# The end of a three-layer kernel: the flag's branch, the last chunks' statistics and the last copies rearranged

## The chip, the cores and the metric
The kernel runs on one core of one Trainium2 chip. The metric is the time of one execution on the device in microseconds (us), taken as the median of several runs. A profile of one execution comes with it; its span runs from the first to the last instruction that belongs to the kernel.

## The reference, cut to what matters
The input is x, 4 batches of 2048 tokens of 256 numbers. Three layers are added to it one after the other:

```python
x = x + 0.5 * ffn(layernorm(x), gate_w, w1, b1, w2, b2)
x = x + attn(layernorm(x), Wq, Wk, Wv, Wo)
x = x + 0.5 * ffn(layernorm(x), gate_w, w1, b1, w2, b2)

# ffn: 8 experts, two of them chosen for each token
cap = int(1.25 * N / E)                       # 1280
probs = softmax(x @ gate_w.T); top2_w, top2_idx = top_k(probs, 2)
counts = bincount(top2_idx.reshape(-1), length=E)
keep = counts <= cap                          # an expert with more tokens than cap gives nothing
# attn: 16 heads of 16, each query sees keys within 128, and token 0 sees and is seen by all
```

An expert that more than 1280 of the 16384 choices fall to adds nothing at all. So if all eight experts are over the limit, both ffn layers add zero, and the result is x + attn(layernorm(x)).

## The kernel before, in words
The kernel computes the attention on the bet that no expert is kept, and collects on the way what is needed to see whether the bet holds: the gates' logits of all tokens before the attention (`logits[0]`), and those after it (`logits[1]`) for the first three batches. From these, eleven VectorE operations (ROUTE, L1299) and a matmul with three small operations (COUNT, L1009 and L1333) make one number, `any_kept`. After the attention every engine loads that number (L1510) and branches on it. If it is 0, nothing is left to do. If not, the general path follows: `route`, `experts`, and perhaps the attention once more. With this input the number is 0.

The attention works on groups: 4 batches of 4 groups of 4 heads, 16 groups, each of 16 tiles of 128 tokens. One tile of a group is an item; the program counts time in quarters of an item, 256 quarters for a batch. Each event has a quarter at which it is begun, read from tables such as `OUT_AT`, and every engine issues its instructions in the order of the quarters (`stages` and `schedule`). An event waits on semaphores for what it needs; the order itself is fixed.

For every item TensorE computes the scores twice. A (L951) serves the row maxima, taken by VectorE (L1447). B (L985) is turned into probabilities by ScalarE (L1128), whose band edges GpSimd cuts (L1237, L1242). PV (L1003) multiplies them by the values into `o_bank`. After every fourth item the bank is copied to `o_raw` (COPY_OUT: ScalarE L1141, and VectorE L1368 for the last six of the 64 quartets), turned by TensorE (TURN, L1023), and added, divided and stored in `attn` by VectorE (OUT_ADD, OUT_RECIP, OUT_MULT: L1476, L1483, L1494).

When all groups of a batch are done, its tokens go through a last stage in 4 chunks of 512 ("LATE"): TensorE turns `attn` (TURN_ATTN, L809, two halves p = 0 and 1), a copy brings it to `attnT` (ScalarE L1069; VectorE L1360 for the last batch), TensorE projects it (PROJECT, L823, four tiles), VectorE adds the residual in `x_ring` (L1355), SyncE stores the chunk (L750). For the second layer's logits VectorE also takes each tile's mean and variance (MOMENTS, L1287 and L1289), and GpSimd derives the logits (RSTD, L1155 to L1185). The four chunks of the last batch have start quarters of their own (`LATE_AT_END`), and the rest of the plan in common with the other batches (`LATE`).

PSUM has eight banks: three for A, two for B, one for PV's sums, and two (`misc`) that TURN, TURN_ATTN, PROJECT, the projections of the next batch (QK, VALUES), the turning of the maxima (L961) and the first token's row (FIRST, L884 among it) share. Which of the two banks a piece gets follows from the order of the quarters: the one that was emptied first.

At the end of the attention's block SyncE waits until all stores have landed (L751 to L754). The block ends with a barrier of all engines (L680), `reset()` follows with another barrier that clears the semaphores (L154), then the load of the flag and the branch.

Of the kernel before, what the change touches and what calls it, by code (L numbers as in the profile page):

```python
# [48 lines left out]
def build(nc, x, wqk, wback, wv, wo, gate, w1, b1, w2, b2, consts, x1, out):  # L49
    ctx = ExitStack()  # L50
    with ctx:
# [318 lines left out]
        def window(j):  # L370
# [19 lines left out]
        OPENING = {'ORDER_HEADS': -55, 'WBACK': -52, 'FOLD': 174, 'K_ONES': 45,  # L390
                   'FILL': 20, 'QK_APART': 1, 'STACK': 4, 'STACKS': 12}
        LATE_AT = (99, 115, 131, 146)
        LATE_AT_END = (51, 66, 83, 100)
        LATE = {'LOAD': -6, 'TURN_ATTN': 1, 'PROJECT': ((7, 8, 10, 10), (12, 12, 14, 14)),
                'BASE': 0, 'MOMENTS': (12, 17, 19, 21), 'RSTD': 23, 'STORE': 19}
        OUT_AT = (0, 0, 3, 3, 0, -1, -1, 0, 2, -1, 1, 0, 0, 0, 3, 4)
        OUT = {'TURN': 0, 'ADD': 0, 'RECIP': 1, 'MULT': 1}
        MAX_AT = {'KEY0': -1, 'TURN_MAX': 1, 'MAX': 2, 'PIECES': 3, 'P0': -1, 'EXP0': 6}

        def stages(nb, first):  # L400
# [15 lines left out]
            for b in range(nb):  # L416
                for c in range(4):
                    early = BATCH * b + EARLY_AT[c] if b else EARLY_AT_OPENING[c]
                    late = BATCH * (b + 1) + (LATE_AT if b < nb - 1 else LATE_AT_END)[c]
                    order.append((early + EARLY["MOMENTS"][0], "EARLY", b, c, early))  # L420
                    order.append((late + LATE["MOMENTS"][0], "LATE", b, c, late))
            order = [item[1:] for item in sorted(order, key=lambda item: item[0])]
            for i, (phase, b, c, at) in enumerate(order):
                plan = EARLY if phase == "EARLY" else LATE
                end(at + plan["LOAD"] if b or phase == "LATE" else -96, "LOAD", i)
                if phase == "LATE":
                    for p in range(2):
                        begin(at + LATE["TURN_ATTN"], "TURN_ATTN", i, p)
                        opening(at + LATE["TURN_ATTN"] + 1, "TURN_ATTN_IN", i, p)
                        for part, quarter in enumerate(LATE["PROJECT"][p]):  # L430
# [4 lines left out]
                    end(at + LATE["BASE"], "BASE", i)  # L435
                    end(at + LATE["STORE"], "STORE", i)
                for t in range(4):
                    quarter = plan["MOMENTS"][t]
                    if (phase, b, c) == ("LATE", nb - 1, 3):
                        quarter = LATE["PROJECT"][t // 2][KC * (t % 2) + KC - 1] + 1  # L440
                    end(at + quarter, "MOMENTS", i, t)
                end(at + plan["RSTD"], "RSTD", i)
# [58 lines left out]
            if first:  # L501
# [10 lines left out]
            return order, opens, begins, ends  # L512

        ROUTE_OPS = 11
# [56 lines left out]
        def attend(nb, dram, batch_at, tiles_at, first):  # L571
# [104 lines left out]
            def stacked(x):  # L676

                return 16 * STACK_DMAS * (x // 4 + 1)

            with nc.Block() as block:  # L680
                @block.sync
                def _(sp):
# [346 lines left out]
                def _(act):  # L1029
# [4 lines left out]
                    for kind, *n in events:  # L1034
# [28 lines left out]
                        elif kind == "TURN_ATTN_IN" and not drained(kind, n[0]):  # L1063
# [80 lines left out]
                def _(pool):  # L1144
                    for kind, *n in events:
                        if kind == "RSTD":
                            i, = n
                            phase, b, c, _ = order[i]
                            tiles = slice(4 * c, 4 * c + 4)
                            pool.wait_ge(S["moments_ready"], 4 * i + 4)  # L1150
                            if i:
                                pool.wait_ge(S["shift_ready"], i)
                            if i >= 2 and order[i - 2][0] == "EARLY":
                                pool.wait_ge(*normed(i - 2))
# [442 lines left out]
```

## Time and profile before

| what | us |
|---|---|
| median of 3 runs | 867.27 |
| lowest and highest of them | 866.34, 868.48 |
| the profiled execution, its own time | 864.91 |
| span of its profile | 862.9 |

The profile lists for each engine its busy time and each group of equal instructions. PE is TensorE, PEld its weight load, DVE VectorE, ACT ScalarE, POOL GpSimd, SP SyncE. A letter q behind an engine's name (PEldq, SPq) means its sequencer: waits, barriers, branches and the issue of transfers. A gap before an instruction stands in square brackets, with what ended it behind the arrow. L with a number is the line of the kernel.

### The profile page before, as it was taken

To read this page: it belongs to the slowest core of one execution; us is meant where nothing else is said; L and a number is where in the kernel's file an instruction comes from. 1 tells how busy PE (TensorE), PEld (TensorE's weight loads), DVE (VectorE), ACT (ScalarE), POOL (GpSimd) and SP (SyncE) were. 2 spreads that over 40 slices of the span, in tenths; PEclk is the share of its full clock that TensorE was granted. 3 is DMA by queue.
4 is the path that set the end of the run, shared out by engine and by line. 5 is a ranking of instruction groups with operands and counts; after the bars stand their busy time and mean duration, and the time that the engine had idled before them with its cause. 6 is when DMAs were issued, how large, how long until landed. Compare 5 with 4: busy or idle time off the path is not lost.

```text
span 862.9 us, 50601 instructions
## 1 busy us (share of the span) xinstructions
PE 816.7 (95%) x21504; PEld 609.6 (71%) x21505; DVE 751.2 (87%) x2814; ACT 633.3 (73%) x1416; POOL 487.2 (56%) x874
## 2 busy tenths in 40 slices
PE   9798999999999999999999999999999999999894
PEld 8555667677777777667778777667777777766672
DVE  7798799998987899998988799998988789999865
ACT  2248978998777667898777676899777756788850
POOL 3212556775554466766555465866554455756863
PEclk9899999999999999999999999999999999999998
DMA  7531224342213334342222344442222244220122
GB/s 230 98 94 64 68 76 130 96 126 64 84 54 98 110 110 159 116 129 64 87 67 70 97 127 140 148 108 85 70 77 64 95 119 140 92 74 31 55 67 87
DMA packets 93190, 83.50 MB, mean 97 GB/s; under 512 B 17568, under 2 KB 92192, under 8 KB 92960
## 3 DMA queue, kind: packets, MB, share of 16 engines
q1 hardware_dynamic: 91360, 78.91, 29.9%
q8 instruction: 171, 2.80, 1.4%
q10 hardware_dynamic: 1600, 1.31, 0.9%
q14 instruction: 59, 0.48, 0.2%
HBM read 20.66 MB, written 8.39 MB: 34 GB/s over the span
## 4 chain that ended last, share of the span: by engine, by line
PE 69%; DVE 12%; ACT 11%; issue 4%; POOL 2%; DMA 1%; SPq 1%; POOLq 0%; ACTq 0%; DVEq 0%
PE bank L1003 13%; PE bank L951 12%; PE bank L985 11%; PE bank L840 11%; PE bank L855 6%; PE bank L823 5%; DVE bank L1447 5%; ACT probs L1128 5%; PE bank L1023 3%; PE bank L809 2%; PE bank L761 2%; ACT pieces L1078 1%; PE bank L776 1%; DVE stats L1287 1%; ACT k_stack L1132 1%
## 5 line engine op out<-in xcount | busy, mean ns | idle before, releaser
L1128 ACT ACTIVATE probs<-bank 128x384 f32<-128x384 f32 (+1 forms) x1024 | 459.5, 481 | 142.1 <-PE bank L985 125.3
L1447 DVE CUSTOM_DVE_ANT_0 bank<-bank,con 128x288 f32<-128x288 f32 x1024 | 494.8, 519 | 55.9 <-PE bank L951 47.7
L951 PE MATMUL bank<-k_stack,q_stack 96*32 96x288 bf16 x4096 | 326.2, 289 | 9.9 <-DVE row_max L1447 6.0
L985 PE MATMUL bank<-q_stack,k_stack 99*32 99x288 bf16 (+2 forms) x4096 | 319.4, 284 | 11.6 <-ACT probs L1128 7.3
L1003 PE MATMUL bank<-probs,v_sb 128*32 128x128 f32 x5888 | 305.6, 272 | 4.1 <-issue 1.4
L1237 POOL TENSOR_SCALAR_AFFINE_SELECT probs<-probs 128x512 f32<-128x512 f32 x240 | 155.0, 646 | 174.8 <-ACT probs L1128 174.4
L1003 PEld LDWEIGHTS bank<-probs,v_sb 128*32 128x32 f32 x5888 | 193.0, 110 | 38.1 <-issue 5.2
L951 PEld LDWEIGHTS bank<-k_stack,q_stack 96*32 96x32 bf16 x4096 | 127.1, 96 | 73.3 <-DVE row_max L1447 21.0
L985 PEld LDWEIGHTS bank<-q_stack,k_stack 99*32 99x32 bf16 x4096 | 123.9, 94 | 70.5 <-ACT probs L1128 44.5
L1242 POOL TENSOR_SCALAR_AFFINE_SELECT probs<-probs 128x512 f32<-128x512 f32 x240 | 153.4, 639 | 19.2 <-ACT probs L1128 19.2
L840 PE MATMUL bank<-xnT,wqk_sb 128*32 128x256 f32 x2048 | 161.5, 386 | 0.6 <-DVE neg_max L1469 0.5
L1447 DVE DVE_READ_ACCUMULATOR2_ANT row_max<- 128x1 f32 x1024 | 145.2, 142 | 0.0
L1225 POOL TENSOR_TENSOR pieces<-rest,pieces 128x512 bf16<-128x512 f32 x64 | 74.5, 1163 | 63.1 <-ACT pieces L1093 61.0
L855 PE MATMUL bank<-wv_sb,xnT 128*32 128x272 f32 x1024 | 83.5, 393 | 1.7 <-ACT v_sb L1100 1.1
L823 PE MATMUL bank<-wo_sb,attnT 128*32 128x264 f32 x1024 | 72.7, 386 | 2.3 <-DVE attnT L1360 1.0
L840 PEld LDWEIGHTS bank<-xnT,wqk_sb 128*32 128x32 f32 x2048 | 65.5, 112 | 6.5 <-ACT v_sb L1100 1.2
L1078 ACT ACTIVATE pieces<-bank 128x512 bf16<-128x512 f32 x64 | 38.3, 598 | 24.3 <-PE bank L840 23.5
L1375 DVE TENSOR_TENSOR rest<-bank,pieces 128x512 f32<-128x512 f32 x64 | 44.1, 689 | 4.1 <-ACT pieces L1078 3.9
L1287 DVE BATCH_NORM_STATS2 stats<-x_ring 128x6 f32<-128x256 f32 x112 | 47.2, 421 | 0.2
L1093 ACT ACTIVATE pieces<-rest 128x512 bf16<-128x512 f32 x64 | 40.6, 634 | 7.6 <-DVE rest L1375 7.5
L1023 PE MATMUL bank<-con,o_raw 128*32 128x68 f32 x2048 | 44.1, 223 | 1.4 <-ACT o_raw L1141 1.0
L823 PEld LDWEIGHTS bank<-wo_sb,attnT 128*32 128x32 f32 x1024 | 33.5, 109 | 14.6 <-issue 2.6
(123 smaller groups left out, 730.9 us busy)
## 6 DMA issues: line engine op xcount, KB each, us to landing
q_stack<-pieces SPq DMA_DIRECT2D x384, 64.0 KB, 2.7
k_stack<-pieces SPq DMA_DIRECT2D x364, 64.0 KB, 2.7
x_ring<-in_x SPq DMA_DIRECT2D x28, 512.0 KB, 4.9
out_x<-x_ring SPq DMA_DIRECT2D x16, 512.0 KB, 4.1
attn<-in_x SPq DMA_DIRECT2D x4, 512.0 KB, 5.8
wback_sb<-in_wback SPq DMA_DIRECT2D x8, 256.0 KB, 6.3
k_stack<-pieces ACTq DMA_DIRECT2D x20, 64.0 KB, 3.6
q_stack<-neg_max SPq DMA_DIRECT2D x48, 16.0 KB, 2.2
```

Of the source, the lines that this page charges most:

```text
L823: last = pe.matmul(bank_of("PROJECT", i, t)[SP * s:SP * (s + 1), 0:D + E], attnT[:, t // 2, k, at:at + SP], wo_sb[:, k, :], start=(k == 0) ...
L840: last = pe.matmul(bank_of("QK", g, c)[SP * s:SP * (s + 1), 256 * half:256 * (half + 1)], wqk_sb[:, g % NG, k, SP * s:SP * (s + 1)], xnT[: ...
L855: last = pe.matmul(bank_of("VALUES", b, t)[SP * s:SP * (s + 1), 0:D + HD], xnT[:, k, at:at + SP], wv_sb[:, k, :], start=(k == 0), stop=(k ...
L951: last = pe.matmul(a_ring[i % len(a_ring)][SP * s:SP * (s + 1), 0:WIN], q_stack[g % 2][0:KROWS, h, q:q + SP], k_stack[g % 2][0:KROWS, h, q ...
L985: last = pe.matmul(score_bank(i)[SP * s:SP * (s + 1), start:final], k_stack[g % 2][0:SROWS, h, WINDOW + P * j + SP * s:WINDOW + P * j + SP ...
L1003: last = pe.matmul(o_bank[SP * h:SP * (h + 1), P * (i % 4):P * (i % 4 + 1)], v_sb[:, j, VW * head:VW * head + SP], probs[:, j % 4, h, P * ...
L1023: last = pe.matmul(bank_of("TURN", n)[SP * s:SP * (s + 1), HG * VW * i:HG * VW * (i + 1)], o_raw[:, at:at + SP], take, start=True, stop=True)
L1128: act.activation(probs[:, j % 4, h, c0:c1], score_bank(i)[:, c0:c1], ACT.Exp, scale=LOGIT_SCALE).then_inc(S["exp_ready"], 1)
L1225: pool.tensor_tensor(pieces[i % 2][:, 2, :], rest[:, :], pieces[i % 2][:, 1, :], ALU.subtract).then_inc(S["piece3_ready"], 1)
L1237: pool.affine_select(out=part, in_=part, compare_op=ALU.is_ge, fill=0.0, base=0, pattern=[[0, HG], [1, P]], channel_multiplier=-1).then_in ...
L1242: pool.affine_select(out=part, in_=part, compare_op=ALU.is_ge, fill=0.0, base=0, pattern=[[0, HG], [-1, P]], channel_multiplier=1).then_in ...
L1447: dve.tensor_tensor_reduce(out=a_ring[i % len(a_ring)][:, 0:WIN], in0=a_ring[i % len(a_ring)][:, 0:WIN], in1=mask, scale=1.0, scalar=con[: ...
```

## The change
- The statistics (MOMENTS) and logits (RSTD) of chunks 1, 2 and 3 of the last batch are no longer computed in the attention. They are computed in the general path (`take_left_out`), which the branch enters only if an expert is kept. `any_kept` doesn't use them.
- SyncE's wait for the stores leaves the attention's block. It stands now in the Else branch of the flag, and in `take_left_out`. The `reset()` after the attention goes; one stands at the end of either branch.
- The last COPY_OUT and the first half of the last chunk's copy to `attnT` are ScalarE's.
- The last batch has a plan of its own, `LATE_END`, with new quarters for its loads, turns, projections, statistics and stores; `LATE_AT_END`, `OUT_AT` (used in every batch), the routing's start and the count's place get new numbers.

The code of MOMENTS and RSTD moves into the functions `moments` and `deviations` without other edits.

```diff
-        LATE_AT_END = (51, 66, 83, 100)
+        LATE_AT_END = (52, 68, 85, 102)
         LATE = {'LOAD': -6, 'TURN_ATTN': 1, 'PROJECT': ((7, 8, 10, 10), (12, 12, 14, 14)),
                 'BASE': 0, 'MOMENTS': (12, 17, 19, 21), 'RSTD': 23, 'STORE': 19}
-        OUT_AT = (0, 0, 3, 3, 0, -1, -1, 0, 2, -1, 1, 0, 0, 0, 3, 4)
+        LATE_END = {'LOAD': -22, 'TURN_ATTN': 0, 'PROJECT': ((6, 6, 8, 9), (12, 15, 15, 15)),
+                    'BASE': -2, 'MOMENTS': (12, 16, 16, 23), 'RSTD': 35, 'STORE': 24}
+        COUNT_AT = 16
+        OUT_AT = (0, 0, 0, 3, -1, -1, -1, 3, 0, 3, 1, 0, 0, 0, 3, 0)
...
+        def left_out(first, nb, phase, b, c):
+            return first and phase == "LATE" and b == nb - 1 and c > 0
...
-                plan = EARLY if phase == "EARLY" else LATE
+                plan = EARLY if phase == "EARLY" else LATE if b < nb - 1 else LATE_END
...
-                for t in range(4):
+                for t in range(0 if left_out(first, nb, phase, b, c) else 4):
...
-                end(at + plan["RSTD"], "RSTD", i)
+                if not left_out(first, nb, phase, b, c):
+                    end(at + plan["RSTD"], "RSTD", i)
...
-                at = BATCH * nb + 7
+                at = BATCH * nb + ROUTE_AT          # 6
...
-                end(max(at + 4 * ROUTE_OPS, BATCH * nb + 4 * LAG_B) + 4, "COUNT")
+                end(max(at + 4 * ROUTE_OPS, BATCH * nb + 4 * LAG_B) + COUNT_AT, "COUNT")
...
             def drained(kind, n):       # true: VectorE copies, false: ScalarE
                 if kind == "COPY_OUT":
-                    return 4 * n + 3 + LAG_PV > NT * NG * nb
-                return order[n][1] == nb - 1
+                    return 4 * n + 3 + LAG_PV > NT * NG * nb and n < 4 * NG * nb - 1
+                return order[n[0]][1] == nb - 1 and (order[n[0]][2] < 3 or n[1] == 1)
...
+            def take_left_out():
+                kept = [i for i, (phase, b, c, _) in enumerate(order) if left_out(first, nb, phase, b, c)]
+                with nc.Block() as block:
+                    @block.sync
+                    def _(sp):
+                        await_stores(sp)
+                    @block.vector
+                    def _(dve):
+                        for i in kept:
+                            for t in range(4):
+                                moments(dve, i, t)
+                    @block.gpsimd
+                    def _(pool):
+                        for i in kept:
+                            deviations(pool, i)
+                reset()
...
-                    for m in range(3):
-                        laps = [lap for s, lap in store_of.values() if s is S[f"stored{m}"]]
-                        if laps:
-                            sp.wait_ge(S[f"stored{m}"], max(laps))
+                    if not first:
+                        await_stores(sp)
...
+            if first:
+                return await_stores, take_left_out
             reset()
...
-        attend(B, x, ..., True)
+        await_stores, take_left_out = attend(B, x, ..., True)
         any_expert = nc.values_load(any_kept[0:1, 0:1], min_val=0, max_val=1)
         with nc.If(any_expert != 0):
-            reset()
+            take_left_out()
             route(logits[0], flags_of[0])
...
+            reset()
+        with nc.Else():
+            await_stores(nc.sync)
             reset()
```

## Rows read from the trace of the kernel before

**Rows 1.** The page, busy time, share of the span and number of instructions.
```profile
PE 816.7 (95%) x21504; PEld 609.6 (71%) x21505; DVE 751.2 (87%) x2814; ACT 633.3 (73%) x1416; POOL 487.2 (56%) x874
```

**Rows 2.** TensorE's waits, whole span: us in total, times, longest.
```profile
PE bank L1023 <- ACT o_raw L1141: 1.0, 5, 0.3
...
PE bank L884 <- DVE attn L1494: 1.0, 3, 0.3
```

**Rows 3.** Timeline of TensorE from 841: start us, us, instructions merged.
```profile
840.80 0.84 PE L1003 MATMUL bank<-probs,v_sb 128*32 128x128 f32 x24
842.19 1.99 PE L823 MATMUL bank<-wo_sb,attnT 128*32 128x264 f32 x32 [0.55 <-DVE attnT L1360]
844.80 1.10 PE L823 MATMUL bank<-wo_sb,attnT 128*32 128x264 f32 x16 [0.63 <-DVE x_ring L1355]
845.69 0.69 PE L1023 MATMUL bank<-con,o_raw 128*32 128x68 f32 x32
846.54 1.10 PE L823 MATMUL bank<-wo_sb,attnT 128*32 128x264 f32 x16 [0.16 <-DVE x_ring L1355]
847.78 1.12 PE L809 MATMUL bank<-con,attn 128*128 128x128 f32 x8
849.39 4.20 PE L823 MATMUL bank<-wo_sb,attnT 128*32 128x264 f32 x64 [0.50 <-DVE attnT L1360]
```

**Rows 4.** Busy time of TensorE in one stretch: us, busy (instructions), clock, DMA.
```profile
841.64:853.59 11.95, 9.91 (x169) 1.00 0.31 100
```

**Rows 5.** Timeline of VectorE, 840 to 854.
```profile
840.78 0.16 DVE L1335 TENSOR_SCALAR within<-bank 1x16 f32<-1x16 f32 x1 [0.85 <-PE bank L1013]
...
841.35 1.29 DVE L1360 COPY attnT<-bank 128x512 f32<-128x512 f32 x2
...
843.64 0.67 DVE L1368 COPY o_raw<-bank 128x512 f32<-128x512 f32 x1
...
853.93 0.40 DVE L1355 TENSOR_TENSOR x_ring<-bank,x_ring 128x264 f32<-128x264 f32 x1
```

**Rows 6.** Groups of equal instructions on VectorE from 840 to 855.1.
```profile
L1287 DVE BATCH_NORM_STATS2 stats<-x_ring 128x6 f32<-128x256 f32 x10 | 4.2, 419 | 0.2
```

**Rows 7.** Timeline of GpSimd from 855.
```profile
855.10 0.23 POOL L1155 TENSOR_SCALAR var_eps<-mean_var 128x4 f32<-128x4 f32 x1 [1.59 <-DVE mean_var L1289]
...
857.35 0.24 POOL L1185 TENSOR_TENSOR all_logits<-late_move,rstd 128x32 f32<-128x32 f32 x1
```

**Rows 8.** Waits of SyncE from 850.
```profile
SPq L680 <- DMA out_x<-x_ring: 2.5, 1, 2.5
```

**Rows 9.** The store's line from 800: duration ns min/median/max, first and last start.
```profile
L750 SPq DMA_DIRECT2D out_x<-x_ring x4: 383/384/384, 829.5 to 854.4; - x4
...
DMA to landing us min/median/max: 2.9/3.6/4.4
```

**Rows 10.** Lines of the end, same columns: block's barrier, clearing barrier, branch.
```profile
L680 SPq COMPARE_BRANCH  x1: 43/43/43, 857.4 to 857.4; - x1
L680 SPq DRAIN  x1: 7/7/7, 857.5 to 857.5; - x1
...
L680 PEldq EVENT_SEMAPHORE  x1: 51/51/51, 857.8 to 857.8; - x1
...
L154 PEldq EVENT_SEMAPHORE  x1: 51/51/51, 858.7 to 858.7; - x1
...
bacc.py:44 PEldq COMPARE_BRANCH  x1: 3454/3454/3454, 859.5 to 859.5; - x1
...
bacc.py:44 SPq COMPARE_BRANCH  x1: 45/45/45, 859.6 to 859.6; - x1
```

**Rows 11.** ScalarE's copies to o_raw in the body, same columns.
```profile
L1141 ACT ACTIVATE o_raw<-bank x58: 591/593/605, 98.7 to 792.4; 128x512 f32<-128x512 f32 x58
```

**Rows 12.** Timeline of SyncE and TensorE from 798.
```profile
800.74 1.09 SPq L712 DMA_DIRECT2D x_ring<-in_x  x2
...
806.56 0.43 PE L1003 MATMUL bank<-probs,v_sb 128*32 128x128 f32 x8 [1.41 <-issue]
```

More of the change, by code:

```diff
@@ L427, in stages @@
                     for p in range(2):
-                        begin(at + LATE["TURN_ATTN"], "TURN_ATTN", i, p)
-                        opening(at + LATE["TURN_ATTN"] + 1, "TURN_ATTN_IN", i, p)
-                        for part, quarter in enumerate(LATE["PROJECT"][p]):
+                        begin(at + plan["TURN_ATTN"], "TURN_ATTN", i, p)
+                        opening(at + plan["TURN_ATTN"] + 1, "TURN_ATTN_IN", i, p)
+                        for part, quarter in enumerate(plan["PROJECT"][p]):
                             t, k = divmod(part, KC)
@@ L507, in stages @@
                     opening(OPENING["FOLD"] + 16 * half + 1, "FOLD_IN", half)
[L508 removed]
+                at = BATCH * nb + ROUTE_AT
                 for op in range(ROUTE_OPS):
                     end(at + 4 * op, "ROUTE", op)
[L511 removed]
+                end(max(at + 4 * ROUTE_OPS, BATCH * nb + 4 * LAG_B) + COUNT_AT, "COUNT")
             return order, opens, begins, ends
+        ROUTE_AT = 6
         ROUTE_OPS = 11
@@ L678, in stacked, with moments @@
                 return 16 * STACK_DMAS * (x // 4 + 1)
+            def moments(dve, i, t):
+                phase, b, c, _ = order[i]
+                if t == 0 and phase == "EARLY":
+                    dve.wait_ge(*x_loaded(i))
+                if t == 0 and i >= 2:
+                    dve.wait_ge(S["shift_ready"], i - 1)
+                if phase == "LATE":
+                    dve.wait_ge(*emptied("PROJECT", i, t))
+                if 4 * i + t >= 4:
+                    dve.wait_ge(S["moments_ready"], 4 * i + t - 3)
+                dve.bn_stats(stats[:, t, :], x_tiles(i)[:, t, :]).then_inc(S["stats_ready"], 1)
+                dve.wait_ge(S["stats_ready"], 4 * i + t + 1)
+                dve.bn_aggr(mean_var[:, i % 2, t, :], stats[:, t, :]).then_inc(S["moments_ready"], 1)
@@ new lines, in await_stores @@
+            def await_stores(sp):
+                for m in range(3):
+                    laps = [lap for s, lap in store_of.values() if s is S[f"stored{m}"]]
+                    if laps:
+                        sp.wait_ge(S[f"stored{m}"], max(laps))
+            def take_left_out():
[14 more added lines that the diff above has]
+                reset()
@@ L1062, in _ @@
                                            ACT.Copy).then_inc(free_sem("XT", i, p), 1)
-                        elif kind == "TURN_ATTN_IN" and not drained(kind, n[0]):
+                        elif kind == "TURN_ATTN_IN" and not drained(kind, n):
                             i, p = n
@@ L1146, in _ @@
                         if kind == "RSTD":
[L1147 to L1154, printed above, removed]
@@ L1155, in _ @@
-                            pool.tensor_scalar(var_eps[:, :], mean_var[:, i % 2, :, 1], EPS, None, ALU.add)\
-                                .then_inc(S["eps_added"], 1)
-                            if phase == "EARLY":
-                                if b >= 2:
-                                    pool.wait_ge(S["shift_ready"], late_index[b - 2, c] + 1)
-                                pool.tensor_scalar(neg_mean[:, b % 2, tiles], mean_var[:, i % 2, :, 0], -1.0, None,
-                                                   ALU.mult).then_inc(S["move_ready"], 1)
@@ L1188, in _ @@
+                            deviations(pool, *n)
                         elif kind == "FILL":
@@ L1276, in _ @@
                         if kind == "MOMENTS":
[L1277 to L1289 removed]
+                            moments(dve, *n)
                         elif kind == "NORM" and on_vector(n[0]):
@@ L1356, in _ @@
                                .then_inc(free_sem("PROJECT", i, t), 1)
-                        elif kind == "TURN_ATTN_IN" and drained(kind, n[0]):
+                        elif kind == "TURN_ATTN_IN" and drained(kind, n):
                             i, p = n
```

98 lines of the change are left out of this document (50 added, 48 removed).

## The prediction
> **What bounds the kernel now.** First the busy shares: TensorE is busy for 816.7 of 862.9 us [rows 1], so in the body an edit on another engine pays only where it removes a TensorE wait. The list of TensorE's waits says how little is there around the output turns, the pieces of the body that are moved: eight waits of at most 0.3 us, 2.0 us together [rows 2]. The end is another stage. The last multiplications with the probabilities (L1003) end at 840.80 + 0.84 = 841.64, and no attention is left but four pieces of chunk work: project chunk 2 (L823, four tiles), turn the last output quartet (L1023), turn chunk 3 (L809), project chunk 3 [rows 3]. The table of stretches shows TensorE busy for only 9.91 of the 11.95 us from 841.64 to 853.59 [rows 4]; each gap is named in the timeline: 0.55 for attnT, 0.63 and 0.16 for x_ring (a bank to be emptied), about 0.15 before the turn of chunk 3, 0.50 for attnT again [rows 3]. All of them are VectorE. Its timeline shows why: it waits 0.85 us for the count (L1335) before it may copy attnT at 841.35, copies o_raw only at 843.64 although its input was complete at 841.64, and ten statistics, 4.2 us [rows 6], stand with their aggregates between its copies [rows 5]. The last addition ends at 853.93 + 0.40 = 854.33.
>
> From 854.33 to 862.9 no matrix work is left, 8.6 us. Two things run side by side first: GpSimd's last deviations, from 855.10 to 857.59 [rows 7], and the last store, issued at 854.4 for 0.38 us [rows 9]; SyncE waits 2.5 us for its landing [rows 8] and leaves that wait at 857.4. Then comes a chain of single steps [rows 10]: the block's barrier lets TensorE go at 857.8, the barrier that clears the semaphores at 858.7, the flag is loaded, and TensorE's branch over the unused experts starts at 859.5 and takes 3.454 us, to 862.9. Outside the span lie 864.91 - 862.9 = 2.0 us.
>
> **The change, part by part.** *Work between 841.64 and 854.33.* Twelve statistics and twelve aggregates (chunks 1 to 3) and three sets of deviations go; ten of each stand in the stretch read above. I worked out TensorE's new order from the new quarter numbers, counted from the last batch's end at 1024: turn chunk 2 at 85, last multiplications to 90, project tile 0 at 91, the last output turn at 92, tile 1 at 93 and 94, the count at 96, tiles 2 and 3 at 97 to 100, turn chunk 3 at 102, its tiles at 108 to 119. Let E be the end of the last multiplications.
> - Tile 0, E to E+1.0: its attnT was turned before, and the count no longer stands ahead of VectorE's copy, so the 0.55 wait goes.
> - Output turn, E+1.0 to E+1.7: the copy of o_raw is now ScalarE's, which is idle after its last exponential, at 0.593 us [rows 11]; it is there by E+0.75. If ScalarE were not free, it would cost 0.67 on VectorE [rows 5].
> - Tile 1 to E+2.7, the count 0.2, tile 2 needs the bank of the output turn, which VectorE frees after its add, reciprocal and multiply (about 1.3 us with issue) at E+3.0: a gap of 0.2. Tile 3 to E+5.05; nothing stands before its bank now.
> - Turn of chunk 3: its first half follows at once, the second waits for the addition of tile 3 (0.43 + 0.15 of hand-over): gap 0.1; end E+6.25.
> - Copies of attnT: ScalarE takes the first half while TensorE turns the second, so projecting starts near E+6.45, a gap of 0.2 in place of 0.50.
> - Four tiles at 4.20/4 each (the 4.20 us row shows them back to back, so here nothing is won), to E+10.65; hand-over 0.15 and addition 0.40: E+11.2.
>
> Before, that distance was 854.33 - 841.64 = 12.7. Gain 1.5; with the count (0.2) no longer ahead of E, less than that since it comes back behind E: I take 1.6 in all. The lower bound is 0.2 (only the statistic that delays the last addition, which could start at 853.59 + 0.15 and starts at 853.93); the upper one is all idle time, 11.95 - 9.91 = 2.0, plus those 0.2. What is late next is TensorE itself, at 1.05 us a tile. GpSimd ends early: its last set is gone.
>
> *End.* SyncE no longer waits in the block. From the last addition's end: issue done +0.5 (854.4 + 0.38 - 854.33), block's end on SyncE +0.1, barrier +0.45 (857.4 to 857.8 [rows 10]), then without the clearing barrier the flag load and the branch, 858.7 to 862.9 = 4.2; then in the Else branch SyncE's wait, long met (the store lands at about +3.0, the branch ends at +5.25), and the clearing barrier, 857.8 to 858.7 = 0.9. Sum 6.15 in place of 8.6: gain 2.4. The clearing barrier has only moved; what is won is landing and deviations, which the load and the branch now cover. Two things no row shows. What SyncE's drain at the block's end does with a store in flight: in the rows it took 7 ns after the landing, so 0 to 2.5; I take 0, since that 7 ns row is the nearest. And a branch beside store traffic: 3.454 on idle queues is the one row, so 0 more to another 3.454 if the Else's few instructions need a second fetch; I take 0, since the one row shows one fetch.
>
> The Trainium skill ("Runtime: NRT & Kernel Launch", Instruction fetch mechanics) says that a taken branch whose target lies outside the two pages held forces a fetch by DMA before anything runs. The 3.454 us row on TensorE agrees; the 45 ns row on SyncE shows the branch alone. Against the change speaks "Trainium Kernel Development and Optimization", Key Constraints: transfers of all queues share the same 16 DMA engines and interleave; by it the fetch, now beside a 512 KB store, would be longer than 3.45, and the sum smaller by the part of the store that is still to move.
>
> *The loads* go from 6 to 22 quarters ahead, so three follow at 800.74 instead of two [rows 12]; behind them on SyncE stand only stores. Chunk 3's load waits for chunk 0's store (landing 2.9 to 4.4 [rows 9]) ahead of chunk 1's store: neither is near the end. Right after the two loads TensorE stands 1.41 us for nothing that is named [rows 12]. A third load may lengthen that by half (0.7) or leave it; I take 0.
>
> *The body.* Six of sixteen output turns move by 1 to 4 quarters in each of four batches, 24 in all. The one moved from 0 to -1 stands where others have waits on o_raw (five, 1.0 together, at most 0.3 [rows 2]): 4 x 0.2 = 0.8 lost. The one moved from -1 to 3 gets out of the way of the first-row matmuls (L884 waits for attn three times, 1.0 together [rows 2]): 1.0 won. The others trade places between banks. I take 0, with -2 and +2 as ends; the deviation of one set from quarter 74 to 87 and the routing one quarter earlier lie beside TensorE's 95% [rows 1] and count nothing; uncovered, a set would be the 2.5 us between the last statistic and 857.59.
>
> Sum: 1.6 + 2.4 = 4.0 on a profiled execution of 864.91, which lies 2.4 below the median of 867.27; taken off that median: 863.3.
>
> **Rivals.** *The drain or the fetch gives the end back*: either the landing is waited for after all, and of the end's 2.4 nothing is left (865.7), or the fetch takes 1.5 longer beside the store (864.8) or comes twice (866.7). For it: neither case is in the trace. Against: the drain's 7 ns, and one branch row that already includes one fetch. *The reordered tail does not pay*: a bank claimed in the new order by the wrong piece leaves the waits; 1.6 falls to 0.2, 864.7. *The body gains too*: the 1.0 at L884 without the losses, and part of the gaps beside the other moved turns; 2 us more, 861.3. *Slower*: the moved output turns each wait, or make their bank's next user wait, 0.33, what the three at L884 are [rows 2]: 24 x 0.33 = 7.9, 867.3 - 4.0 + 7.9 = 871.2. It decides from (4.0 + 2.6)/24 = 0.27 a turn. Against: there are two banks, and most turns at the same offsets show no wait in the list.
>
> **How the numbers follow.** A measurement of this kernel tells about 0.3% (2.6 us) from no change: faster is under 864.7. Forecast (gain 3 to 5, 862.3 to 864.3): 0.52. Drain or fetch: 0.16, nearly all "same". Tail does not pay: 0.10, on the border, a third of it faster. Body gains too: 0.15. Slower: 0.07. Faster 0.52 + 0.15 + 0.03 of the border case = 0.70; same 0.23; slower 0.07. The range leaves out the slower case and the tip of the best: 860.8 to 866.7.
>
> **What would show it.** Right: between the last L1003 and the last addition about 11.2 us with TensorE idle under 1 us; the copy of o_raw on ScalarE within 0.8 us of E; the block's barrier released about 1.0 us after the last addition; a branch near 3.45 us, then one clearing barrier, the span's end 6.2 us after the last addition. Wrong: SyncE's drain ends only with the landing; a branch over 4.5 us or two of them; L1023, L884 or L961 with more waits than before in the middle batches; a gap well over 1.41 us at 805.

## The result and the profile after

The changed kernel takes 860.79 us (median), the kernel before 867.27: the ratio is 0.9923, with an interval from 0.9895 to 0.995, that is 6.7 us less (4.3 to 9.1). The forecast was 863.3, the range 860.8 to 866.7: the sign was right, the gain is 6.7 where 4.0 were forecast, and the time lies 0.01 us below the range. The profiled execution took 860.79 us, its span is 858.7.

Below, E is again the end of the last multiplications with the probabilities (L1093 in the new file), T the end of the last addition (L1393).

Busy shares on the page of the changed kernel, against [rows 1]:
```profile
PE 811.9 (95%) x21504; PEld 611.7 (71%) x21505; DVE 743.2 (87%) x2788; ACT 634.7 (74%) x1418; POOL 481.3 (56%) x856
```
TensorE's timeline after E, changed kernel, against [rows 3]:
```profile
839.79 0.62 PE L1093 MATMUL bank<-probs,v_sb 128*32 128x128 f32 x16
840.22 1.07 PE L913 MATMUL bank<-wo_sb,attnT 128*32 128x264 f32 x16
841.12 0.68 PE L1113 MATMUL bank<-con,o_raw 128*32 128x68 f32 x32
842.04 1.10 PE L913 MATMUL bank<-wo_sb,attnT 128*32 128x264 f32 x16 [0.24 <-DVE x_ring L1393]
842.93 0.25 PE L1103 MATMUL bank<-counts,ones 128*1 128x8 f32 x4
843.22 1.99 PE L913 MATMUL bank<-wo_sb,attnT 128*32 128x264 f32 x32
845.14 1.33 PE L899 MATMUL bank<-con,attn 128*128 128x128 f32 x8
846.57 3.82 PE L913 MATMUL bank<-wo_sb,attnT 128*32 128x264 f32 x64
```
ScalarE's timeline there, and VectorE's last addition (against [rows 5]):
```profile
840.47 0.60 ACT L1231 ACTIVATE o_raw<-bank 128x512 f32<-128x512 f32 x1 [5.47 <-PE bank L1093]
845.83 0.60 ACT L1159 ACTIVATE attnT<-bank 128x512 f32<-128x512 f32 x1 [4.76 <-PE bank L899]
```
```profile
850.45 0.43 DVE L1393 TENSOR_TENSOR x_ring<-bank,x_ring 128x264 f32<-128x264 f32 x1 [0.46 <-PE bank L913]
```
E is 839.79 + 0.62 = 840.41 and T is 850.88: 10.5 us in place of 12.7. Of the five gaps that the prediction read from [rows 3] one of size is left, 0.24 before tile 1, which waits for tile 0's addition; before the last four tiles 0.1 is left (846.47 to 846.57). ScalarE has o_raw copied 0.66 after E.

The lines of the end (ns min/median/max, first and last start), against [rows 10]: the block's barrier, the flag's load, the branch, the Else branch's wait for the stores, the clearing barrier.
```profile
L772 SPq DRAIN  x1: 128/128/128, 851.4 to 851.4; - x1
...
L772 PEldq EVENT_SEMAPHORE  x1: 51/51/51, 851.7 to 851.7; - x1
```
```profile
L1550 SPq TENSOR_LOAD <-any_kept x1: 1092/1092/1092, 851.8 to 851.8; - x1
...
L1550 PEldq TENSOR_LOAD <-any_kept x1: 1079/1079/1079, 851.8 to 851.8; - x1
L1550 SPq FUSED_REGOPS  x1: 194/194/194, 852.9 to 852.9; - x1
L1550 SPq SEQ_ASSERT  x1: 37/37/37, 853.1 to 853.1; - x1
```
```profile
L1567 PEldq COMPARE_BRANCH  x1: 3382/3382/3382, 853.0 to 853.0; - x1
L1567 SPq COMPARE_BRANCH  x1: 50/50/50, 853.5 to 853.5; - x1
```
```profile
L750 SPq EVENT_SEMAPHORE  x2: 17/22/28, 857.9 to 857.9; - x2
```
```profile
L154 PEldq DRAIN  x1: 78/78/78, 856.4 to 856.4; - x1
...
L154 PEldq EVENT_SEMAPHORE  x1: 51/51/51, 858.7 to 858.7; - x1
```
SyncE's drain takes 128 ns with the store in flight, and the barrier opens at 851.7, 0.8 after T: the landing is not waited for. But TensorE is at the clearing barrier at 856.4, and SyncE executes its first instruction of the Else branch only at 857.9. The distance from T to the span's end is 7.8; the forecast was 6.15, and before it was 8.6.

Ahead of E something else is to be seen. TensorE's waits over the whole span, changed kernel (total, times, longest), against [rows 2]:
```profile
PE bank L1093 <- issue: 4.8, 5, 3.0
...
PE bank L1051 <- DVE attn L1532: 1.6, 2, 0.8
...
PE bank L1113 <- ACT o_raw L1231: 1.6, 8, 0.3
```
The waits of the first row's matmuls (L884) on attn are gone; the turn of the maxima (L1051) waits instead. And the stand (idle time of TensorE that no semaphore explains, "issue") of 1.41 near 806 [rows 12] is 3.0 now. The first line is TensorE's timeline, the second SyncE's. The third is the table of stretches for the 6.8 us behind the stand: length, busy time and number of instructions of PE, PEld, DVE, ACT and POOL, then TensorE's granted clock, the DMA engines' share and GB/s.
```profile
804.39 0.66 PE L1093 MATMUL bank<-probs,v_sb 128*32 128x128 f32 x8 [3.01 <-issue]
```
```profile
796.93 2.19 SPq L804 DMA_DIRECT2D x_ring<-in_x  x3
```
```profile
804.39:811.20 6.81, 6.80 (x148) 5.73 (x151) 3.41 (x6) 3.36 (x9) 2.98 (x5) 0.56 0.03 6
```
After standing 3 us TensorE works at a granted clock of 0.56: most of that stretch at the lower level (1.2 GHz). This trace is the worst one: behind the stands of 2.5 us or more at this place in the other traces of this document the clock of such a stretch is 0.75 to 0.80, behind the shorter ones 1.00 in all but one.

One trace is one execution. In the table stand the means of all traces of the kernel before (six) and of the changed kernel and two near copies of it (five in all; body_back and loads_back, below), in us. "First exp" is the first exponential of a group.

| stage | before | after | difference |
|---|---|---|---|
| start to first exp | 75.7 | 76.0 | +0.3 |
| to first exp of group 14 | 694.7 | 692.6 | -2.1 |
| to first exp of group 15 | 33.5 | 32.6 | -0.8 |
| to E | 38.3 | 39.8 | +1.5 |
| E to T | 12.7 | 10.5 | -2.2 |
| T to the span's end | 8.7 | 7.8 | -0.9 |
| span | 863.6 | 859.3 | -4.3 |

The third, fifth and sixth differences are steady, since these stages vary by 0.5 at most in nearly all traces. The exception is one trace of the kernel before whose stand near 801 fell into the third stage (34.4); the other five have 33.3, so that this difference is -0.7 without it. The first, second and fourth move by up to 4, 5 and 3 us between executions of the same kernel.

### The profile page after: what moved, and what is told of

It reads as the page before. It is cut to its first block, busy times and chain, and to the rows that moved or that the text cites. A ratio compares the mean times of both kernels' runs of the same rounds, so it can differ in the third digit from the quotient of the medians.

```text
span 858.7 us, 50541 instructions
## 1 busy us (share of the span) xinstructions
PE 811.9 (95%) x21504; PEld 611.7 (71%) x21505; DVE 743.2 (87%) x2788; ACT 634.7 (74%) x1418; POOL 481.3 (56%) x856
## 4 chain that ended last, share of the span: by engine, by line
PE 67%; DVE 13%; ACT 9%; issue 4%; SPq 2%; DMA 2%; POOL 1%; ACTq 0%; DVEq 0%
PE bank L1093 14%; PE bank L1075 11%; PE bank L1041 11%; PE bank L930 10%; PE bank L945 6%; PE bank L913 6%; DVE bank L1485 6%; ACT probs L1218 4%; PE bank L1113 3%; PE bank L899 2%; DVE stats L698 1%; SPq L830 1%; ACT xn L1131 1%; PE bank L866 1%; DVE row_max L1485 1%
## 5 line engine op out<-in xcount | busy, mean ns | idle before, releaser
L1075 PE MATMUL bank<-q_stack,k_stack 99*32 99x288 bf16 (+3 forms) x4096 | 320.3, 286 | 11.4 <-ACT probs L1218 8.3
L1093 PE MATMUL bank<-probs,v_sb 128*32 128x128 f32 x5888 | 307.6, 273 | 6.0 <-issue 4.8
L1093 PEld LDWEIGHTS bank<-probs,v_sb 128*32 128x32 f32 x5888 | 194.2, 111 | 38.4 <-issue 8.2
L930 PE MATMUL bank<-xnT,wqk_sb 128*32 128x256 f32 x2048 | 157.7, 379 | 0.6 <-DVE neg_max L1507 0.5
L1168 ACT ACTIVATE pieces<-bank 128x512 bf16<-128x512 f32 x64 | 38.3, 598 | 20.3 <-PE bank L930 19.1
L1304 POOL TENSOR_TENSOR glob_term<-v_all,p 128x272 f32<-128x272 f32 x64 | 41.6, 649 | 2.2 <-DVE v_all L1454 1.8
```

The source lines that it names most:

```text
L930: last = pe.matmul(bank_of("QK", g, c)[SP * s:SP * (s + 1), 256 * half:256 * (half + 1)], wqk_sb[:, g % NG, k, SP * s:SP * (s + 1)], xnT[: ...
L1075: last = pe.matmul(score_bank(i)[SP * s:SP * (s + 1), start:final], k_stack[g % 2][0:SROWS, h, WINDOW + P * j + SP * s:WINDOW + P * j + SP ...
L1093: last = pe.matmul(o_bank[SP * h:SP * (h + 1), P * (i % 4):P * (i % 4 + 1)], v_sb[:, j, VW * head:VW * head + SP], probs[:, j % 4, h, P * ...
```

## The experiments

Each ratio is to runs of the kernel before taken beside it on the same chip.

**Which part pays.** The kernel before again; the changed kernel again; the new end alone; the statistics alone (left out altogether in this kernel, and so not computed in the general path either); statistics and end together with the old order and copies; the changed kernel with its last copies on VectorE.
```diff
 end_only:    LATE_AT_END, OUT_AT, ROUTE_AT, COUNT_AT, drained as before; LATE_END = LATE
+             left_out(...): return False
 stats_only:  (in the kernel before)
+             left_out = first and phase == "LATE" and b == nb - 1 and c > 0
 stats_end:   tables and drained as before, left_out as in the change
 copies_old:
-             return 4 * n + 3 + LAG_PV > NT * NG * nb and n < 4 * NG * nb - 1
-             return order[n[0]][1] == nb - 1 and (order[n[0]][2] < 3 or n[1] == 1)
+             return 4 * n + 3 + LAG_PV > NT * NG * nb
+             return order[n[0]][1] == nb - 1
```


> The kernel before, unchanged, as a yardstick for what differs from execution to execution. Theory A (the clock in the opening differs by chance): ratio to the kernel before 1.000; its profile shows in the first 80 us another number of stretches at the lower clock than the profile of before had (0.76 granted from 26 to 40 us), and the first exponential lies elsewhere than 77.6 us. Theory B (the opening differs because of the change): the first exponential is at 77.6 again, and the granted clock from 26 to 40 is 0.76 again.

> The changed kernel unchanged, for a second profile and more times. Both theories: 10.48 us from the last multiplications to the last addition, 7.7 from there to the end, ratio 0.992. Theory A (the differences ahead of the last multiplications are chance): the start of the first exponential differs from 74.0 by the number of stretches at the lower clock in the opening, and TensorE's stand near 801 is sometimes near 1.3 us instead of 3.0. Rival (the stand belongs to the changed code): 3.0 us again.

> The kernel before with one part of the change: the wait for the stores and the clearing barrier go behind the branch. Statistics, order and copies are the old ones. Theory A (GpSimd's last deviations end the block at 857.6 as before, the landing at 857.4 was just hidden by them): barrier, load, branch and clearing barrier in another order, 8.6 us from the last addition to the span's end as before, ratio 1.000, less 0.4 us at most. Rival (the landing alone was the price): 2 us faster, 0.9975.

> The kernel before without the statistics and deviations of the last batch's chunks 1 to 3; order, copies and end are the old ones. It leaves those statistics out altogether (the general path, which this input doesn't enter, would lack them). Theory A (what the traces show behind the last multiplications is the whole gain, the rest is chance before it): 12.69 us from the last multiplications to the last addition falls to about 11.7 (the waits for x_ring go, those for attnT stay), 8.55 us from there to the span's end to 8.3, since the landing is waited for; ratio 0.9985. Theory C (the missing statistics also take something away ahead of the last multiplications, in the executions that are timed): ratio 0.995 or lower.

> The kernel before with the statistics of chunks 1 to 3 moved to the general path and with the new end (wait for the stores and clearing barrier behind the branch); tables, order and copies are the old ones. Theory A: last multiplications to last addition as without the statistics (about 11.7 us), from there 7.7 us as in the changed kernel; ratio 0.998. Theory C: ratio 0.994. What it lacks to the changed kernel is the new order and ScalarE's copies.

> The changed kernel with all of the last copies on VectorE again. Theory A: the wait of the output turn grows by 0.2 to 0.4 us and the one before chunk 3's projection to about 0.5, so 10.48 us become 11.0 and the kernel is 0.5 us slower than the changed one, ratio to the kernel before about 0.993. Rival (the copies on ScalarE are idle detail): 10.48 us stay.

| kernel | us | ratio, 95% | E to T | T to end |
|---|---|---|---|---|
| before_again | 865.28 | 1.000 (0.9974 to 1.0026) | 12.69 | 8.54 |
| end_only | 867.18 | 0.9992 (0.9961 to 1.0023) | 12.69 | 9.78 |
| stats_only | 865.35 | 0.998 (0.9957 to 1.0003) | 11.17 | 8.72 |
| stats_end | 864.11 | 0.9975 (0.9948 to 1.0001) | 11.17 | 7.85 |
| copies_old | 861.36 | 0.9932 (0.9907 to 0.9957) | 10.67 | 8.20 |
| after_again | 860.94 | 0.9912 (0.9879 to 0.9944) | 10.48 | 8.07 |

The distance from E to T is the same to 0.02 in all traces of one order, and so it splits cleanly: the statistics 1.52, the new order 0.50, the copies on ScalarE 0.19. The statistics are worth more than was expected of stats_only (11.7), the copies less than was expected of copies_old (11.0). TensorE's stretch in stats_only, against [rows 3]:
```profile
847.59 0.68 PE L1025 MATMUL bank<-con,o_raw 128*32 128x68 f32 x32
848.44 1.10 PE L825 MATMUL bank<-wo_sb,attnT 128*32 128x264 f32 x16 [0.16 <-DVE x_ring L1357]
...
851.18 3.82 PE L825 MATMUL bank<-wo_sb,attnT 128*32 128x264 f32 x64 [0.38 <-DVE attnT L1362]
```
Without the statistics the 0.63 before the output turn is gone, and the last four tiles take 3.82 in place of 4.20: the row of 4.20 held waits behind the statistics that it did not list. In copies_old the last tiles still wait 0.20 for attnT, the price of VectorE's copy:
```profile
843.89 3.82 PE L913 MATMUL bank<-wo_sb,attnT 128*32 128x264 f32 x64 [0.20 <-DVE attnT L1398]
```
The new end alone wins nothing: GpSimd's deviations still end 3.25 us behind T and hold the block, and the Else branch then puts SyncE's late arrival and a clearing barrier behind it (9.78). It needs the statistics gone.

**What the end costs.** The wait for the landing back in the block; and the flag loaded without its check against 0 and 1.
```diff
 landing_waited:
-                    if not first:
-                        await_stores(sp)
+                    await_stores(sp)
 no_assert:
-        any_expert = nc.values_load(any_kept[0:1, 0:1], min_val=0, max_val=1)
+        any_expert = nc.values_load(..., skip_runtime_bounds_check_because="...")
```


> The changed kernel with SyncE's wait for the stores inside the attention's block again; all else is the changed one. Theory A (the landing runs beside barrier, load and branch, and the flag's load takes 1.1 instead of 0.5 us because the store is in flight): load 0.5 us, 9.8 us from the last addition to the span's end instead of 7.8, 2 us slower than the changed kernel. Rival (what ends last is not the landing, so nothing is won by taking it out): 7.8 us stay.

> The changed kernel without SyncE's check of the flag's bounds between its load and its branch. Theory A (SyncE branches 0.5 us after the others, and its code comes 4.2 us later, so it is the last at the clearing barrier): SyncE's branch 0.5 us earlier, 7.8 us become 7.3, 0.5 us faster than the changed kernel, which is less than the runs can tell apart, so the trace decides. Rival (SyncE's code comes when the other four have theirs, whenever it asks): 7.8 us stay.


Measured: landing_waited 861.85 us, 0.9955 (0.9933 to 0.9977), T to the end 9.75; no_assert 860.78 us, 0.9945 (0.9923 to 0.9966), T to the end 6.85. Flag loads of landing_waited, where the store has landed before:
```profile
L1549 SPq TENSOR_LOAD <-any_kept x1: 479/479/479, 852.8 to 852.8; - x1
...
L1549 PEldq TENSOR_LOAD <-any_kept x1: 486/486/486, 852.8 to 852.8; - x1
```
SyncE's branch and its first instruction behind it, no_assert (its T is 853.91):
```profile
L1568 SPq COMPARE_BRANCH  x1: 50/50/50, 855.9 to 855.9; - x1
```
```profile
L750 SPq EVENT_SEMAPHORE  x2: 17/22/28, 859.8 to 859.8; - x2
```
Both costs of the new end are shown in the traces; in the runs' times no_assert is not faster than the changed kernel. The load of the flag takes 1.08 beside the store and 0.48 without it: 0.6. SyncE's check sets its branch 0.5 behind the others'; without it the branch is at T + 2.0 in place of T + 2.6, and SyncE arrives 1.1 earlier after T. That is more than the 0.5 that was expected: 0.6 comes from the branch, the rest from the way behind it, 3.8 us in this one trace and 4.1 to 4.7 in the twelve others with the new end, for which no run shows a cause. In each of these kernels SyncE needs about 4 us from its 50 ns branch to the next instruction (853.5 to 857.9; 855.9 to 859.8), as TensorE does within its 3.4 us branch.

**The loads and the turns.** Two loads again near 801; the old turns in the first three batches; the old turns everywhere but for the last one.
```diff
 loads_back:
-        LATE_END = {'LOAD': -22, ...
+        LATE_END = {'LOAD': -6, ...
 body_back:
+        OUT_AT_BODY = (0, 0, 3, 3, 0, -1, -1, 0, 2, -1, 1, 0, 0, 0, 3, 4)
+        ... (OUT_AT_BODY if b < nb - 1 else OUT_AT)[4 * g + q]
 out_back:    the same, and
+        OUT_AT = (0, 0, 3, 3, 0, -1, -1, 0, 2, -1, 1, 0, 0, 0, 3, 0)
```


> The changed kernel with the last batch's loads 6 quarters ahead again, so that two loads and not three follow the maxima. Theory A (the third load stretches TensorE's stand at 801 us from 1.41 to 3.01 us, and the low clock from 803 to 810 follows from it): the stand is near 1.4 us, no low clock behind it, last multiplications with the probabilities about 2 us nearer to the start of the last group, kernel 2 to 3 us faster than the changed one. Rival (the stand is a matter of where the code lies, not of the loads): still about 3 us, and no faster.

> The changed kernel with the old places of the output turns in the first three batches; the last batch keeps the new ones. Theory A (the moved turns cost 0.4 us from 74 to 755 us, as the two traces have it): 0 to 1 us faster than the changed kernel. Rival (the moved turns are where the gain beyond the forecast comes from): 2 to 3 us slower than the changed kernel, with the lead lost evenly over the batches.

> The changed kernel with the old places of the output turns in all four batches, but for the very last turn. Theory A (the moved turns of the last batch shorten the stretch from the first exponential of the last but one group to that of the last group from 33.3 to 32.65 us, those of the other batches do nothing that lasts): 33.3 us again in that stretch, 10.48 us behind the last multiplications as before, 0.7 to 1.0 us slower than the changed kernel, ratio to the kernel before 0.9935. Rival (the stretch is shortened by the last batch's own plan, not by the turns): 32.65 stays, ratio 0.9925.


Measured: loads_back 859.6 us, 0.9923 (0.9891 to 0.9956); body_back 861.08, 0.9919 (0.9891 to 0.9946); out_back 863.03, 0.9957 (0.9933 to 0.9982). The third load is not what lengthens the stand: loads_back stands 3.04. In the first three batches the moved turns exchange one wait for another, and their net is nothing: body_back and out_back have the waits of the first row on attn again, where one batch passes into the next (in out_back near 204, 403 and 605), and the changed kernel waits 0.81 twice at L1051 (403 and 605) in their place. The line is out_back's:
```profile
PE bank L975 <- DVE attn L1533: 1.0, 3, 0.4
```
In the last batch the moved turns pay: from group 14 to 15 it takes 32.6 in after and body_back and 33.4 in out_back, with the same number of multiplications. 0.33 of the 33.4 is a wait for a DMA (q_stack) that comes and goes between executions of one kernel; against the 33.3 of the kernel before the gain is 0.7. The waits of the first row are not its cause, since none of them lies in that stretch and body_back, at 32.6, has them too; which of the small waits there makes it was not tried. In the runs' times out_back is 2.2 above the changed kernel, with intervals that overlap.

**More traces.** The steady stages alone do not reach the measured difference. Here are four more traces of the kernel before and one of the changed kernel.


> The kernel before once more, for a third profile. Theory A (with the opening's clock and the stand near 801 taken out, the kernel before needs 36.4 us from the last group's first exponential to the last multiplications, 33.3 us for the interval ahead of it, 12.69 and 8.55 behind): these four again. Rival (they differ from execution to execution): other numbers.

> Theory chance: the earlier traces of the kernel before were merely short ones; its stages here are those seen (last multiplication to last addition 12.7, that addition to the end 8.5 to 8.7, group 14 to 15 33.3), and a time near its mean of 866.7 shows as longer stands near 801 or more low-clock stretches. Theory stage: one stage of the kernel before is often longer than in its three traces, by 1 to 3, at an equal granted clock, and never so in the kernel after.

> As for the run before it in this call: chance leaves every fixed stage alone, stage shows one of them 1 to 3 longer.

> As for the run before it in this call: chance leaves every fixed stage alone, stage shows one of them 1 to 3 longer.

> Both theories: 10.48 from the last multiplication to the last addition, 7.7 to 8.1 behind it, 32.6 from group 14 to 15, and a span near 858.6. Chance wants its stand near 801 to be as long as that of the three kernels before in this call, stage wants nothing of it.


Profiled times 865.99, 865.52, 868.33, 865.77; the changed kernel 859.5. E to T is 12.69 or 12.70 in all four, T to the end 8.5 to 8.9: no fixed stage is longer. The slowest one has its time in stands of TensorE without a named cause, 8.2 us in three lines where the first trace had 2.5 in them; its waits:
```profile
PE bank L951 <- issue: 4.0, 5, 1.7
PE bank L1023 <- issue: 2.5, 3, 1.4
PE bank L1003 <- issue: 1.7, 3, 1.1
```
The stand near 801 is not the chance that was expected of it: the kernel before has 1.1 to 1.4 in four of its six traces, 2.5 and 3.1 in the others; the changed kernel and its two near copies have 2.8 to 3.3 in all five. But the long stand needs neither the new order nor the third load: end_only and stats_only, with the old order and two loads, have 3.1 and 3.3, in one trace each, and stats_end has 1.1. With the changed plan of the last batch all nine traces so far have 2.8 to 3.3.

**The stand near 801.** The records of the DMA queues named it. The page of the changed kernel (packets, MB, share) has a queue of kind "instruction":
```profile
q8 instruction: 172, 2.82, 1.5%
```
That is 16 KB a packet and 66 bytes for each of TensorE's 43,009 matmuls and weight loads: it fits their code. These packets come every 4.6 us (median); in the changed kernel one came at 793.26 and the next at 801.80, 8.5 later, behind the three x loads. DMA queues of the changed kernel from 797.2 to 801.7, and from 801.7 to 801.9:
```profile
q1 hardware_dynamic: 1026, 0.97, 72.5%
q14 instruction: 1, 0.01, 1.1%
```
```profile
q1 hardware_dynamic: 77, 0.07, 112.7%
q8 instruction: 1, 0.02, 32.5%
```
In all eighteen traces of the kernels told of so far the stand ends 2.3 to 2.7 behind the start of such a packet, whether it is short (before: 803.87, end 806.56) or long (801.80, end 804.39).

The same holds for the other stands without a named cause. From 80 us to E the twenty traces of this document have 125 of more than 0.25 us, and every one ends 2.2 to 3.2 behind the start of a q8 packet. By chance about 22% of them would, the share of the whole time that lies so. The longest one of before_5, and the DMA queue from 581.3 to 581.5:
```profile
584.09 0.30 PE L951 MATMUL bank<-k_stack,q_stack 96*32 96x288 bf16 x2 [1.73 <-issue]
```
```profile
q8 instruction: 1, 0.02, 37.1%
```
And each of the twenty branches of TensorE at the end holds one such packet, which starts 1.0 to 1.2 us behind the branch's start (once 1.6); the branch ends 2.3 to 2.8 behind it. So these stands and the branch are waits for code.

Two kernels moved the loads, by a wait on TensorE's progress; no instruction of TensorE and no turn is changed in them:
```diff
+    if first and order[i][0] == "LATE" and order[i][1] == nb - 1 and order[i][2] < 3:
+        sp.wait_ge(S["b_full"], HG * (NT * (NG * nb - 1) + (1, 5, 9)[order[i][2]]))  # loads_apart
+                                                     #     (5, 5, 5)                   loads_burst
```


> The last batch's loads of chunks 0, 1 and 2 no longer leave SyncE together: each waits until the last group's item 1, 5 or 9 has its probabilities' scores (B), some 8 us apart. Theory code fetch: TensorE's code arrives in 16 KB packets about every 4 us; beside the loads one is 8.5 late, and TensorE stands until 2.3 to 2.7 behind that packet. Spread out, a load holds a packet up by 1.5 at most: the stand of 3.0 falls below 1.3, the low-clock stretch behind it goes, from the first exponential of group 15 to the last multiplication it is 36.5 to 37.3 instead of 39.1 to 40.4, and the time is 2 to 3 below the changed kernel's. Rival, the new order of the turns: the stand stays at 2.7 or more near 801, and the time is the changed kernel's.

> The three loads leave together as in the changed kernel, but only when item 5 of the last group has its scores, some 10 us later. Theory code fetch: the stand follows the loads, 2.5 to 3.3 some 3 to 6 behind them, near 815, and is gone at 801; the time is the changed kernel's. Rival: the stand stays near 801.


Measured: loads_apart 858.81 us, 0.9892 (0.986 to 0.9924); loads_burst 859.12 us, 0.9905 (0.987 to 0.994). TensorE's timeline and the stretch behind it in loads_apart, then the stand in loads_burst:
```profile
802.85 0.42 PE L1095 MATMUL bank<-probs,v_sb 128*32 128x128 f32 x8 [0.83 <-issue]
```
```profile
802.85:809.70 6.85, 6.49 (x200) 4.95 (x199) 6.52 (x10) 6.14 (x16) 5.34 (x8) 1.00 0.24 70
```
```profile
802.25 0.43 PE L1095 MATMUL bank<-probs,v_sb 128*32 128x128 f32 x8 [0.55 <-issue]
```
Without the loads at 797 to 801 the stand falls from 3.0 to 0.8 and 0.55, the granted clock behind it stays at 1.00, and from group 15's first exponential to E it takes 36.4 and 36.2 in place of 39.8. So it is shown, by one trace of each of two edits, that the loads' burst at this place makes the long stand. The other half of the expectation failed: the later burst (806.9) did not make a stand of 3 us. The next packet came 6.4 after its predecessor, and the longest gap there, 0.66, is put down to o_raw. So a burst alone is not enough. That it must meet the moment at which code is due fits all this but was not tried further, nor what sets how much code TensorE has in store. The mean of loads_apart is 858.4, that of the changed kernel's runs, taken beside other ones, 860.6: about 2 us less, which these few runs do not settle; the stretch to E, 3.3 shorter, is plain.

The Trainium skill ("Runtime: NRT & Kernel Launch", Instruction fetch mechanics) says that each engine fetches its next block of 16 KiB ahead over a DMA queue of its own, so that crossing into one is mostly hidden. The 16 KB packets of q8 agree (nearly all of those of q14, the other instruction queue, are of 8 KB); beside 1.5 MB of loads the crossing was not hidden but cost 3.0.

## Why the prediction was right and wrong

- **Work between E and T** (forecast 11.2, gain 1.6): right in kind; measured 10.5, gain 2.2, which is the upper bound that the prediction gave. The mis-sized term is "four tiles at 4.20/4 each ... here nothing is won". They take 3.82; the row of 4.20 was not back to back. That is 0.4 of the 0.7 missed; 0.1 is the gap before them, 0.1 in place of 0.2, and the rest lies in the tiles before, which end 4.8 behind E in place of 5.05.
- **End** (forecast 6.15, gain 2.4): the step "then in the Else branch SyncE's wait, long met" failed. It put the Else branch at TensorE's arrival. SyncE arrives 1.5 later, since its branch stands behind the flag's check and its own way behind the branch is longer. The row with SyncE's 45 ns branch was there [rows 10], but what follows it lay behind the old span's end, where no row shows it. With the flag's load, 0.6 slower, and the barrier, 0.25 earlier, this is the whole difference; the gain is 0.9 (means) in place of 2.4. Of the rivals' two causes, drain and fetch, neither came: the drain is 0.13, the branch 3.38. That was in part luck: the store lands 3.0 behind T, and TensorE's code packet starts 3.1 behind T, so that its fetch was hardly beside the store. Whether a store lengthens a fetch, as the prediction feared, no run here tests; that loads hold code up is seen near 801.
- **Loads** (0, risk 0.7 by a third load): the place was right, the mechanism wrong. Not the third load but the burst's holding up TensorE's code counts, and the stretch from group 15's first exponential to E is 1.5 longer in the mean over the traces. It hides a gain there: without the stand itself the stretch is 36.4 before (the three traces that have a short stand in it) and 35.6 in loads_apart and loads_burst, all at a clock of 1.00. Which edit wins this 0.8 was not tried.
- **Body** (0, ends -2 and +2): right for the first three batches, as far as the moved turns go; for the last one the turns give 0.7. No trace shows 24 turns with a wait of 0.33 each, so the slower rival is out. The rival "the body gains too" (861.3) comes nearest to the time, but its mechanism, the waits at L884, is not what gained.
- **The sum**: 4.0 was forecast from 1.6 + 2.4 + 0; the steady stages are 2.2 + 0.9 + 0.7 = 3.8, nearly the same sum with other terms. That its errors cancel (work +0.6, end -1.5, body +0.7) is luck. So what put the time below the range lies where the prediction took 0, in the body. In the traces the spans differ by 4.3. Of the 2.1 won there on the way to group 14, waits for code are 1.7 (4.3 before, 2.6 after, in the mean); but they range from 1.7 to 7.9 in the traces of the kernel before, and from 2.1 to 4.3 in the eleven traces of the changed kernel and its variants, so that this cannot be put down to the change with certainty. Means over all runs differ by 6.3 (867.0, 119 runs, to 860.6, 20 runs), 2 us more than the traces. These 2 us stay open. They are not the moved turns of the first three batches (body_back is as fast), nor another granted clock (0.9925 and 0.9927 in the mean of the runs). Runs of one kernel scatter with a standard deviation of 2 to 3 us, so six traces against five can miss as much by chance. The profiled 864.91 on which the sum was made was itself a short execution, 2 us below the mean.

## What to carry to other kernels

In these traces the branch to the far end of the program costs every engine its own 3.4 to 4.7 us until its next instruction: put into the sum the engine that branches last, not the one whose branch row is long. A long row of merged instructions hides short waits, so compare it with its undisturbed twin before "nothing is won here" is written. A burst of loads can have a price for engines that do not read it: where TensorE stands and no semaphore explains it, look for the instruction packet that starts 2 to 3 us ahead of its next instruction, and try to let the burst wait for progress.

## What had not been expected of the hardware

- SyncE's branch takes 50 ns in its row, and then 3.8 to 4.7 us pass before its next instruction; TensorE's has the whole fetch in the row, 3.36 to 3.92 over all traces.
- Every stand of TensorE of more than 0.25 us without a named cause, 125 in twenty traces, ends 2.2 to 3.2 us behind the start of a 16 KB instruction packet.
- Loading one number into a register takes 0.47 to 0.55 us, and 1.06 to 1.17 while a 512 KB store is under way.
- The opening is a matter of chance in either kernel: the first exponential comes between 73.9 and 77.6 us. With a granted clock of 1.00 from 26 to 47 us it comes at 74.0, with 0.76 at 77.4 to 77.6. With 0.92 it comes at 75.8 to 76.5 where the lower level begins at 26 to 28 us, and at 73.9 to 74.3 where it begins at 39; whether the clock makes the delay is not shown. The same kernel twice (changed kernel, second execution of it):
```profile
26.00:47.00 21.00, 18.29 (x437) 11.80 (x441) 19.56 (x79) 5.12 (x9) 4.28 (x5) 1.00 0.66 108
```
```profile
26.00:47.00 21.00, 18.59 (x356) 11.05 (x356) 16.00 (x64) 3.54 (x6) 3.10 (x4) 0.76 0.58 97
```
Between the first two traces of the two kernels the opening alone made 3.6 us, which a comparison of one trace with one trace would have put down to the change.
